# Attention block on one core: six q/k/v buffers, a kept input tile, and a new slot table

## The reference, cut to what matters

```python
qkv = gn(x) @ qkv_w + qkv_b                       # 196 tokens x 576
attn = (q * scale) @ k.T                          # per head, 196 x 196
attn += rel_h[:, :, :, None] + rel_w[:, :, None, :]   # q times position tables, 14 rows and 14 columns
attn = softmax(attn, axis=-1)
out = (attn @ v) @ proj_w + proj_b                # then x + out
```

## Time and profile before

| | us |
|---|---|
| median of 3 runs | 2341.02 (2326.52 to 2341.86) |
| the profiled execution, its own time | 2339.97 |
| span of its instructions | 2338.2 |
| TensorE matmul busy | 2094.7 (90% of the span) |
| TensorE weight loads busy | 1595.9 |
| VectorE busy | 1653.4 |
| ScalarE busy | 1621.4 |
| GpSimd busy | 714.4 |
| one residual add on GpSimd, mean of 128 | 1.00 |
| one DMA issue of `rel` on SyncE (L358), median of 512 | 0.69 |
| bytes moved | 216.34 MB, mean 93 GB/s |

### The profile page before, as it was taken

How to read it: one execution, slowest core, us unless ns; L and a number is a source line. 1 busy time by engine, 2 the same in 40 slices (tenths; PEclk the granted TensorE clock), 3 DMA queues, 4 the chain that set the end, 5 groups by cost and what they waited for, 6 DMA issues and landing times.

```text
span 2338.2 us, 73485 instructions
## 1 busy us (share of the span) xinstructions
PE 2094.7 (90%) x27904; PEld 1595.9 (68%) x27904; DVE 1653.4 (71%) x3923; ACT 1621.4 (69%) x3713; POOL 714.4 (31%) x1796
## 2 busy tenths in 40 slices
PE   1899999999999989999999999899989999999998
PEld 1677676776767767667667766677766766777765
DVE  5677777667767677777677777677767777777675
ACT  0577777677767667767676777677767776777675
POOL 1233323333333233333233333233223333333230
PEclk9899999999999999999999999999999999999999
DMA  1333434333434333433333443344334343334331
GB/s 47 84 94 95 104 91 105 91 92 91 103 93 97 90 94 93 101 93 93 91 98 91 94 103 96 88 96 100 91 91 102 94 100 93 94 93 103 91 92 47
DMA packets 170550, 216.34 MB, mean 93 GB/s; under 512 B 29783, under 2 KB 138072, under 8 KB 170202
## 3 DMA queue, kind: packets, MB, share of 16 engines
q1 hardware_dynamic: 170202, 211.64, 37.7%
HBM read 117.00 MB, written 57.80 MB: 75 GB/s over the span
## 4 chain that ended last, share of the span: by engine, by line
PE 39%; DMA 33%; SPq 14%; DVE 6%; issue 4%; ACT 3%; POOL 1%; POOLq 0%; ACTq 0%; DVEq 0%
PE ps_m L412 18%; DMA q_st<-mrow 17%; DMA k_dram<-qk_hl 10%; PE ps_sc L538 7%; PE ps_max L525 6%; SPq L375 6%; DMA q_dram<-qk_hl 6%; DVE qk_hl L734 4%; PE ps_o L557 3%; SPq L382 3%; ACT qk_hl L598 2%; SPq L341 2%; SPq L387 2%; PE ps_m L501 2%; DVE rel_hl L776 1%
## 5 line engine op out<-in xcount | busy, mean ns | idle before, releaser
L722 DVE TENSOR_REDUCE mx<-ps_max 98x2 f32<-98x392 f32 x1536 | 819.4, 562 | 232.6 <-PE ps_max L525 215.5
L586 ACT ACTIVATE probs<-ps_sc 98x392 f32<-98x392 f32 x1536 | 714.5, 497 | 232.3 <-PE ps_sc L538 198.2
L525 PE MATMUL ps_max<-k_st,q_st 124*98 124x196 f16 x3072 | 548.9, 261 | 82.4 <-DVE mx L722 82.1
L538 PE MATMUL ps_sc<-q_st,k_st 125*98 125x196 f16 x3072 | 523.3, 252 | 95.6 <-DMA q_st<-mrow 94.1
L776 DVE TENSOR_TENSOR rel_hl<-ps_m,rel_hi 64x504 f16<-64x504 f32 (+1 forms) x768 | 431.4, 562 | 162.0 <-ACT rel_hi L643 152.9
L525 PEld LDWEIGHTS ps_max<-k_st,q_st 124*98 124x98 f16 x3072 | 295.0, 126 | 296.4 <-issue 198.0
L538 PEld LDWEIGHTS ps_sc<-q_st,k_st 125*98 125x98 f16 x3072 | 320.9, 126 | 123.1 <-DMA q_st<-mrow 120.4
L557 PE MATMUL ps_o<-probs,v_st 98*32 98x196 f32 x6144 | 389.6, 340 | 0.5 <-ACT o_sb L578 0.5
L634 ACT ACTIVATE rel_hi<-ps_m,is_lo 64x504 f16<-64x504 f32 (+1 forms) x384 | 223.9, 583 | 189.1 <-PE ps_m L471 185.7
L471 PE MATMUL ps_m<-q_st,rel_st 64*32 64x84 f16 x7168 | 341.6, 266 | 4.8 <-DVE rel_hl L776 4.5
L809 POOL TENSOR_TENSOR msq<-mv 96x2 f32<-96x2 f32 x128 | 24.4, 191 | 1007.1 <-DVE mv L748 1007.1
(11 more groups left out here) (72 smaller groups left out, 3293.8 us busy)
## 6 DMA issues: line engine op xcount, KB each, us to landing
q_st<-q_dram SPq DMA_DIRECT2D x128, 294.0 KB, 3.8
k_st<-k_dram SPq DMA_DIRECT2D x256, 147.0 KB, 3.9
q_dram<-qk_hl SPq DMA_DIRECT2D x128, 147.0 KB, 2.6
k_dram<-qk_hl SPq DMA_DIRECT2D x128, 147.0 KB, 2.7
q_st<-rel_hl SPq DMA_DIRECT2D x256, 73.5 KB
q_st<-rel_hl SPq DMA_DIRECT2D x256, 64.3 KB
xa<-in_x SPq DMA_DIRECT2D x64, 147.0 KB
xd<-in_x SPq DMA_DIRECT2D x64, 147.0 KB
```

Source lines behind the costliest of these rows:

```text
L525: last = nc.tensor.matmul(ps_max[head % 2][0:HT, h * TOK:h * TOK + TOK], q_st[u.r][0:R_MAX, head, h, :], k_st[u.r][0:R_MAX, head, :], star ...
L538: last = nc.tensor.matmul(ps_sc[head % 2][0:HT, kt * TOK:kt * TOK + TOK], k_st[u.r][0:STACK, head, kt * HT:kt * HT + HT], q_st[u.r][0:STAC ...
L586: nc.scalar.activation(probs[head][:, :, :], ps_sc[head % 2][0:HT, 0:2 * TOK].rearrange("p (k t) -> p k t", k=2), ACT.Exp, scale=1.0 / (QS ...
L722: nc.vector.reduce_max(mx[u.r % 2][:, head, :], ps_max[head % 2][0:HT, 0:2 * TOK].rearrange("p (q k) -> p q k", q=2), axis=AX.X).then_inc( ...
```

## The change

There are six buffers for q, k and v stacks in place of four. The input tile `xa` has eight buffers in place of two and is kept until the residual add, which reads it; the load `xd` and its buffers go. One more iteration stands ahead and one more behind (`LEAD`, `TAIL`). All places of jobs, copies, DMAs and GpSimd steps, the order of the jobs and their banks are new. No arithmetic changes.

```diff
+VB = 6
+QB = 6
+XB = 8
-        q_st = [sb(f"q_st{i}", [128, HEADS, 2, HT], F16) for i in range(4)]
-        k_st = [sb(f"k_st{i}", [128, HEADS, TOK], F16) for i in range(4)]
-        v_st = [sb(f"v_st{i}", [HT, 2, HEADS, PW]) for i in range(4)]
+        q_st = [sb(f"q_st{i}", [128, HEADS, 2, HT], F16) for i in range(QB)]
+        k_st = [sb(f"k_st{i}", [128, HEADS, TOK], F16) for i in range(QB)]
+        v_st = [sb(f"v_st{i}", [HT, 2, HEADS, PW]) for i in range(VB)]
-        xa = pair("xa", [HT, 2, C])
+        xa = [sb(f"xa{i}", [HT, 2, C]) for i in range(XB)]
-        xd = pair("xd", [HT, 2, C])
-        LEAD, TAIL = 1, 6
-        MAX_AT, EXP_AT = 28, 40
-        PV_AT = {(0, 0): 44, (0, 1): 45, (1, 0): 49, (1, 1): 51, (2, 0): 54, (2, 1): 54}
-        O_LATER = 1
-        JOBS = [(60, "y", 0, (s_yr, 1, 1)),
-                (3, "qk0", 1, (s_qklo, 2, 1)),
-                (3, "qk1", 0, (s_qklo, 2, 2)),
-                (-9, "xT", 2, (s_xT, 1, 1)),
-                (17, "rel0", 0, (s_rlo, 3, 1)),
-                (41, "mT1", 2, (s_mrow, 2, 2)),
-                (18, "rel1", 1, (s_rlo, 3, 2)),
-                (-5, "g", 2, (s_g, 1, 1)),
-                (56, "ot", 0, (s_on, 1, 1)),
-                (20, "rel2", 1, (s_rlo, 3, 3)),
-                (58, "oT", 2, (s_olo, 1, 1)),
-                (10, "v", 0, (s_v, 1, 1)),
-                (35, "mT0", 1, (s_mrow, 2, 1))]
+        LEAD, TAIL = 2, 7
+        MAX_AT, EXP_AT = 30, 42
+        PV_AT = {(0, 0): 45, (0, 1): 46, (1, 0): 50, (1, 1): 52, (2, 0): 55, (2, 1): 55}
+        O_LATER = 2
+        JOBS = [(36, "mT0", 0, (s_mrow, 2, 1)),
+                (1, "qk0", 2, (s_qklo, 2, 1)),
+                (2, "qk1", 0, (s_qklo, 2, 2)),
+                (63, "y", 2, (s_yr, 1, 1)),
+                (-9, "xT", 1, (s_xT, 1, 1)),
+                (18, "rel0", 0, (s_rlo, 3, 1)),
+                (42, "mT1", 1, (s_mrow, 2, 2)),
+                (19, "rel1", 2, (s_rlo, 3, 2)),
+                (-4, "g", 0, (s_g, 1, 1)),
+                (57, "ot", 0, (s_on, 1, 1)),
+                (21, "rel2", 2, (s_rlo, 3, 3)),
+                (58, "oT", 1, (s_olo, 1, 1)),
+                (11, "v", 0, (s_v, 1, 1))]
-        ACT_LATER = {"qk": 0, "mT": 1, "oT": 0, "xT": 0, "rel": 0, "v": 0, "y": 0}
-        DVE_LATER = {"bn": 2, "g": 0, "ot": 0, "oT": 0, "qk": 0, "rel": 0}
-        POOL_AT = {"mv": -11, "group": -3, "xn": -1, "xhi": 0, "xlo": 0, "y": 63}
+        ACT_LATER = {"qk": 0, "mT": 0, "oT": 0, "xT": 0, "rel": 0, "v": 0, "y": 1}
+        DVE_LATER = {"bn": 3, "g": 0, "ot": 0, "oT": 3, "qk": 1, "rel": 1}
+        POOL_AT = {"mv": -6, "group": -3, "xn": -1, "xhi": 2, "xlo": 5, "y": 82}
-        SP_AT = {"m0": 39, "m1": 46, "rel": 22, "qk_out": 3, "q_in": 3, "k_in": 4, "xd": 55, "out": 69, "xa": -12}
+        SP_AT = {"m0": 39, "m1": 41, "rel": 23, "qk_out": 6, "q_in": 7, "k_in": 6, "out": 80, "xa": -15}
...
-                    u = due(unit, s, SP_AT["xd"])
-                    if u:
-                        src, at = (x_in, u.n) if not layer_of(u, layer) else (x1, u.n - SAMPLES)
-                        wait(sp, s_y, u.n - 1)
-                        sp.dma_start(xd[u.r % 2][:, :, :], tokens(src[bass.ds(at, 1)])).then_inc(s_xd[u.r], 16)
...
-                        wait(sp, s_xT_ps, u.n - 1)
-                        sp.dma_start(xa[u.r % 2][:, :, :], tokens(src[bass.ds(at, 1)])).then_inc(s_x[u.r], 16)
+                        wait(sp, s_y, u.n - XB + 1)
+                        sp.dma_start(xa[u.n % XB][:, :, :], tokens(src[bass.ds(at, 1)])).then_inc(s_x[u.r], 16)
...
-                        wait(act, s_o_ps, (u.n - 3) * GROUPS)
+                        wait(act, s_o_ps, (u.n - VB + 1) * GROUPS)
...
-            for i in range(UNROLL):
+            for i in range(VB):
                 nc.vector.memset(v_st[i][:, :, :, :], VS)
             dve.wait_ge(s_const, 16 * 8)
-            for i in range(UNROLL):
+            for i in range(QB):
                 for head in range(HEADS):
                     nc.vector.tensor_copy(k_st[i][R_REL:STACK, head, :], oh_raw[R_REL:STACK, :])
...
-                        wait_dma(pool, s_xd, u)
-                        nc.gpsimd.tensor_tensor(yo[p2][:, :, :], yr[p2][:, :, :], xd[p2][:, :, :], ALU.add)\
+                        nc.gpsimd.tensor_tensor(yo[p2][:, :, :], yr[p2][:, :, :], xa[u.n % XB][:, :, :], ALU.add)\
```

More of the change, by code:

```diff
@@ L209, in attention_kernel @@
         s_y_ps = sem("s_y_ps")
-        s_xd = sems("s_xd")
         s_yr = sem("s_yr")
@@ L335, in maxima @@
                     wait(sp, s_mrow, unit_.n * 2 + half + 1)
-                    sp.dma_start(q_st[unit_.r][R_MAX:STACK, half * HH:half * HH + HH, :, :],
+                    sp.dma_start(q_st[unit_.n % QB][R_MAX:STACK, half * HH:half * HH + HH, :, :],
                                  mrow[unit_.r % 2][:, half, :]).then_inc(s_m[half][unit_.r], 16)
@@ L357, in iteration @@
                                 p, r0 = 64 * axis + 32 * half, R_REL + RW * axis
-                                sp.dma_start(q_st[u.r][r0:r0 + rows, half * HH:half * HH + HH, :, :],
+                                sp.dma_start(q_st[u.n % QB][r0:r0 + rows, half * HH:half * HH + HH, :, :],
                                              rel_hl[u.r % 2][p:p + rows, :, :]).then_inc(s_rel[u.r], 16)
@@ L368, in iteration @@
                         q_part = q_dram[u.r].rearrange("l d (o h) c t -> (l d) o (h c t)", o=1)
-                        sp.dma_start(q_st[u.r][0:R_REL, :, :, :], q_part.to_broadcast([2 * HD, 2, HEADS * TOK]))\
+                        sp.dma_start(q_st[u.n % QB][0:R_REL, :, :, :], q_part.to_broadcast([2 * HD, 2, HEADS * TOK]))\
                           .then_inc(s_qst[u.r], 16)
@@ L374, in iteration @@
                         for part in range(2):
-                            sp.dma_start(k_st[u.r][2 * HD * part:2 * HD * part + 2 * HD, :, :],
+                            sp.dma_start(k_st[u.n % QB][2 * HD * part:2 * HD * part + 2 * HD, :, :],
                                          k_dram[u.r].rearrange("l d h c t -> d l (h c t)"))\
                               .then_inc(s_kst[u.r], 16)
-                    u = due(unit, s, SP_AT["xd"])
-                    if u:
-                        src, at = (x_in, u.n) if not layer_of(u, layer) else (x1, u.n - SAMPLES)
-                        wait(sp, s_y, u.n - 1)
-                        sp.dma_start(xd[u.r % 2][:, :, :], tokens(src[bass.ds(at, 1)])).then_inc(s_xd[u.r], 16)
                     u = due(unit, s, SP_AT["out"])
@@ L429, in job @@
                             last = nc.tensor.transpose(ps[0:CC, c * TOK + h * HT:c * TOK + h * HT + HT],
-                                                       xa[p2][:, h, c * CC:c * CC + CC], ident[0:HT, 0:HT])
+                                                       xa[u.n % XB][:, h, c * CC:c * CC + CC], ident[0:HT, 0:HT])
                     last.then_inc(s_xT_ps, 1)
@@ L462, in job @@
                             for half in range(2):
-                                q = q_st[u.r][0:R_REL, half * HH:half * HH + HH, :, :]\
+                                q = q_st[u.n % QB][0:R_REL, half * HH:half * HH + HH, :, :]\
                                     .rearrange("p h q t -> p h (q t)")
@@ L525, in iteration @@
                             last = nc.tensor.matmul(ps_max[head % 2][0:HT, h * TOK:h * TOK + TOK],
-                                                    q_st[u.r][0:R_MAX, head, h, :],
-                                                    k_st[u.r][0:R_MAX, head, :],
+                                                    q_st[u.n % QB][0:R_MAX, head, h, :],
+                                                    k_st[u.n % QB][0:R_MAX, head, :],
                                                     start=True, stop=True)
@@ L538, in iteration @@
                             last = nc.tensor.matmul(ps_sc[head % 2][0:HT, kt * TOK:kt * TOK + TOK],
-                                                    k_st[u.r][0:STACK, head, kt * HT:kt * HT + HT],
-                                                    q_st[u.r][0:STACK, head, :, :],
+                                                    k_st[u.n % QB][0:STACK, head, kt * HT:kt * HT + HT],
+                                                    q_st[u.n % QB][0:STACK, head, :, :],
                                                     start=True, stop=True)
@@ L557, in iteration @@
                                 last = nc.tensor.matmul(ps_o[32 * j:32 * j + 32, 0:TOK],
-                                                        v_st[u.r][:, kt, head_of(head), :], p[:, kt, :],
+                                                        v_st[u.n % VB][:, kt, head_of(head), :], p[:, kt, :],
                                                         start=kt == 0, stop=kt == 1)
@@ L647, in iteration @@
                         act.wait_ge(s_v_ps, u.n + 1)
-                        wait(act, s_o_ps, (u.n - 3) * GROUPS)
-                        nc.scalar.copy(v_st[u.r][:, :, :, 0:HD],
```

(2 more changed lines are left out.)

## The result

The changed kernel takes 2873.06 us (median of 4 runs, 2870.33 to 2876.89) against 2337.26 us before: ratio 1.230, 95% interval [1.225, 1.235]. The sign was forecast, the size was not: 2650 us with a range of 2430 to 2750.

A forecast was written before the change was run, and what follows sets the result against it. TensorE was taken to bound the kernel: 15.86 + 2.32 + 0.40 + 1.45 = 20.03 us a unit against 17.58, +304 us over 124 units; with 5.8 + 3 about 2650 us, range 2430 to 2750.

The forecast's parts named there:

- The sign: Whole kernel: the change makes it slower; slower by over 1% was given chance 0.89.
- Old wait on `mrow`: TensorE at head 6: the wait for the maxima that SyncE's `m1` brings goes, -0.73 us a unit.
- `m0` stayed in time: SyncE: `m0` reaches head 0 in time; the rival, `m0` late, up to 1 us a unit more, had chance 0.06.
- The old wait of `ps_max` on `mx`: TensorE in slot 8: the wait for VectorE's maximum moves behind a longer one and is counted out, -0.64 us a unit.
- The ring through bank 0: `g` must wait for VectorE's read of `rel0`, `ot` for its copy `gsm`: +2.32 us a unit, 1.9 to 2.6.
- `mT0` behind `v`: On bank 0, `mT0` one pair behind `v` must wait for the copy `v_st`: +0.40 us, 0.3 to 0.5.
- GpSimd at 0: GpSimd's `xn_lo` is ready about when TensorE comes to `qk0`: 0 us, up to +0.3.
- Preparation: Before TensorE's start: two more `v_st` and 24 more casts into `k_st` on VectorE, +5.8 us once, 4.5 to 6.
- One more iteration at each end: TensorE's last place moves from 60 to 63, three half-filled slots: +3 us once, 0 to 6.
- Clock: TensorE behind the new waits: a fall costing about 1.7 us in 0.85 of the units, +1.45 us a unit, 0 to 2.4.
- The Trainium skill's rule: TensorE's clock falls in every turn of a loop with a recurring wait: 1.7 us in all units, about 30 us more.

The follow-up runs named there:

- e4: The kernel before with SyncE's list alone changed, `m1` issued earlier and `q_in` and `k_in` behind it: 2199.56 us, ratio 0.940.
- e1: The kernel before with one number changed, job `g` on bank 0 instead of bank 2: 2821.28 us, ratio 1.205.
- e2: The changed kernel with one number changed, job `g` on bank 1 instead of bank 0: 2589.35 us, ratio 1.106.
- e3: The changed kernel with unread matmuls filling its two waits, 5 ahead of `g` and 13 ahead of `ot`: 2470.00 us, ratio 1.055.
- e10: e2 with 11 unread matmuls ahead of `ot`: 2422.04 us, ratio 1.026.
- e5: The kernel before with two small DMAs ahead of each `m1`, so that the wait at head 6 grows: 2483.04 us, ratio 1.047.
- e6: The changed kernel with 5 unread matmuls in the wait ahead of `g` alone, the wait ahead of `ot` left idle: 2817.55 us, ratio 1.188.
- e13: e6 with 24 narrow matmuls behind `ot` replaced by 15 wide ones in each unit: 2566.76 us, ratio 1.088.
- e8: The kernel before with six q, k and v buffers, eight kept input tiles and no load `xd`, all places as they were: 2239.82 us, ratio 0.945.
- e14: e5 with the 12 wide matmuls of `v` replaced by 16 of at most 32 columns: 2452.80 us, ratio 1.039.
- e12: e4 with the kept input tile (eight buffers) and four q, k and v buffers: 2201.51 us, ratio 0.933.
- e11: The changed kernel with 16 unread matmuls directly behind `ot`, the waits left idle: 3249.48 us, ratio 1.376.

## Why the prediction was wrong, and where it was right

- *Old wait on `mrow`*, -0.73 us a unit: right, and shown twice (e4, and its absence in the profile after). `m0` stayed in time. The old wait of `ps_max` on `mx` (-0.64) went too, from 82.1 to 0.4 us.
- *The ring through bank 0*, +2.32 us: right. 272.1 us over 123 to 126 units is 2.2 us; e1 and e2 make and unmake it with one number.
- *`mT0` behind `v`*, +0.40: 0.06 in the changed kernel and 0.32 with the clock up (e3).
- *GpSimd at 0*: right while the ring is there (10.6 us, 4 times), 0.6 us a unit without it (e10).
- *Preparation*, +5.8 us: TensorE started 5.6 us later. *One more iteration at each end*, +3 us: no run shows it apart.
- *Clock*, +1.45 us a unit: **this is the step that failed.** It was "half of 3.4, about 1.7 us" in 0.85 of the units. The changed kernel leaves 21.8 - 15.9 - 2.2 - 0.1 = 3.6 us a unit for it, and e3 shows it directly: 403 us over 128 units is 3.1 us, and with the 0.25 us that `mT0` then waits longer, 3.4. How often it falls was nearly right (124 stretches for 0.85 x 124 = 105). How long it stays low was not: 8.2 us for 3.4. I had taken the length from falls at head 6, where `oT` and `v` follow; the new wait stands ahead of `ot`, `rel2` and products with v. e5 and e6 show that the length goes with the place, and e13, where one step of work was swapped behind the same wait, that it goes with the work behind it. Even for head 6 the length was low: the 17 falls of the kernel before between 110 and 2280 us last 4.2 us on the mean. On the other side, half of the low time was too high a price for it, 4.0 us a unit by that rule for 3.4 to 3.6: not all matmuls take twice as long at half clock (eight products with v 0.88 for 0.54 us).

With 3.6 in the place of 1.45 the sum is 2650 + 124 x 2.15 = 2917, and 2873 was measured; `mT0` at 0.06 takes 42 of the 44 us between. The upper bound for that term, 2.4 us, was too low as well: it let every second fall be a double one. The earlier trace rows already held a fall of 6.8 us, and nothing in the profile before showed a fall at the new place. The sign was no luck: it hung on the ring, which is there as laid out.

The Trainium skill's rule that was weighed there ("TensorE: Matmul & The Clock Gate", section "HAM oscillation — how this bites in real kernels"), a fall in every turn, is told of a loop whose waits last about 3 to 5 us. The waits here are shorter, and for them the traces decide: 124 low stretches in 128 units behind waits of 1.5 us agree with it, but 92 behind the 1.3 us of e2 and 60 behind the 1.45 us (mean) of e5 do not.

It is argued and not shown that the same holds for e1, whose `ot` has the same work behind it. It stays open which property of the narrow work matters: e13 changed width, type and number of the matmuls at once, and only e14 changed the width within one type, together with the amount of work. It is open too how much of e5's smaller number of falls comes from the scatter of its waits and how much from the place: waits of 1.5 us and a little more were followed by a fall in 19 of 29 cases there, in 110 of 123 in e6 and in 83 of 123 in e13.

## What to carry to other kernels

Price a new wait of TensorE by the place it stands at: look at what the engine runs behind it, and at how long the clock stayed low behind waits in that same place; a price taken from another place was off by a factor of 2.4 here. Follow every shared bank or buffer round: here one number in a table cost 20%, and a DMA placed four entries earlier in SyncE's list gave 6%. When a new layout comes with several edits, run the halves alone: one half of this change was 5% faster by itself (e8), and the version to keep is the old table with `m1` ahead of `q_in` and `k_in` (e4: 2199.56 us, 0.940), which the kept tile doesn't improve (e12).

## What the runs showed of the hardware that I had not expected

- TensorE's clock stayed at the lower level while TensorE was busy without a gap: 0.50 from 1413 to 1419 us with 6.00 of 6.00 us busy, running products of 32 columns, transposes and then `v`.
- 18 matmuls of 96x128x256 a unit that nobody reads, in waits of 0.67 and 1.51 us, raised the granted clock from 0.823 to 0.997 and shortened the program from 2873 to 2470 us. Sixteen such matmuls behind the wait (e11) lengthened it to 3249 us.
- A little less waiting did more than its length: in e8 the wait on `mrow` went from 0.73 to 0.23 us a unit, which is 64 us, and the low clock from 0.8 to 0.15 us a unit (0.978 to 0.996). The kernel gained 5.5%, 128 us.
- Fifteen wide matmuls in place of 24 narrow ones behind the same wait of 1.51 us halved the low stretches, from 7.8 us (e6) to 3.8 us (e13).
